# Attention probabilities normalised before the transpose, kept in fp32, and multiplied with values as the stationary operand, two heads at a time

## The reference

```python
xn = ln(x, g_norm)
q = (xn @ Wq).reshape(b, n, HEADS, DIM_HEAD).transpose(0, 2, 1, 3)
k, v = split(xn @ Wkv)                      # null key and value are put in front
sim = einsum('bhid,bjd->bhij', q, k) * SCALE + attn_bias    # bias of the null column: null_attn_bias
sim = where(causal or padding mask, neg, sim)
attn = softmax(sim, axis=-1)                # over the null column and 1024 keys
out = einsum('bhij,bjd->bhid', attn, v)
return ln(out @ Wout, g_out)                # added to x by the caller
```

## Time and profile before

| what | value |
|---|---|
| median of three runs | 1751.86 us |
| profiled execution, its own time | 1753.54 us |
| its span | 1751.1 us |
| PE busy (by modelled ends) | 1476.3 us, 84% |
| DVE busy | 1391.8 us, 79% |
| ACT busy | 1241.2 us, 71% |
| POOL busy | 752.5 us, 43% |
| mean granted TensorE clock | 0.965 of 2.4 GHz |

### The profile page before, as it was taken

The page is one execution under the profiler, slowest core; times in us unless marked ns, Lnnn a source line. Parts: engine busy times, 40 slices in busy tenths (PEclk is TensorE's granted clock), DMA queues, the critical chain, the costliest instruction groups (busy, mean ns, idle before and its releaser), DMA issues.

```text
span 1751.1 us, 46745 instructions
## 1 busy us (share of the span) xinstructions
PE 1476.3 (84%) x16377; PEld 1085.6 (62%) x16377; DVE 1391.8 (79%) x3587; ACT 1241.2 (71%) x3512; POOL 752.5 (43%) x1412
## 2 busy tenths in 40 slices
PE   2367778787889999987788888999999799999998
PEld 1255556666667777765666666777777555555555
DVE  4556677877888989977788888899999677777777
ACT  1278888888889999987888888889999533233322
POOL 5546676543433434356554332322231366522222
PEclk9668999999999999999999999999999899999999
DMA  4002111211122213111222111222223000000000
GB/s 136 14 16 62 50 61 50 79 62 52 54 74 86 86 63 109 56 38 38 72 64 74 56 67 65 73 79 86 92 98 98 2 25 19 1 1 1 13 13 25
DMA packets 50442, 96.70 MB, mean 55 GB/s; under 512 B 3332, under 2 KB 27028, under 8 KB 50212
## 3 DMA queue, kind: packets, MB, share of 16 engines
q1 hardware_dynamic: 45504, 90.27, 15.8%
q10 hardware_dynamic: 4708, 3.45, 0.7%
HBM read 91.54 MB, written 2.17 MB: 54 GB/s over the span
## 4 chain that ended last, share of the span: by engine, by line
PE 43%; DVE 19%; ACT 17%; issue 10%; POOL 2%; ACTq 0%; DVEq 0%; POOLq 0%
DVE p_lo L965 7%; PE tp L1307 7%; ACT p_hi L723 6%; DVE biased L881 4%; PE sc L1081 3%; PE sc L1082 3%; PE sc L1083 3%; ACT probs L630 3%; PE sc L1198 3%; ACT q_b L651 3%; PE sc L1199 3%; PE op L1081 2%; PE aux L1081 2%; ACT q_sq L663 2%; PE aux L1083 2%
## 5 line engine op out<-in xcount | busy, mean ns | idle before, releaser
L965 DVE TENSOR_TENSOR p_lo<-tp,p_hi 128x512 f16<-128x512 f32 (+3 forms) x768 | 416.3, 554 | 157.0 <-ACT p_hi L723 150.3
L881 DVE CUSTOM_DVE_ANT_0 biased<-sc,bias,neg_null 128x256 f32<-128x256 f32 (+7 forms) x512 | 411.0, 803 | 3.7 <-PE sc L1199 1.4
L1307 PE MATMUL tp<-ident,probs 128*128 128x128 f32 x2304 | 390.9, 279 | 26.5 <-DVE p_lo L965 23.6
L630 ACT ACTIVATE probs<-biased,neg_max 128x256 f32<-128x256 f32 (+7 forms) x512 | 397.9, 777 | 6.9 <-DVE neg_max L881 5.5
L723 ACT ACTIVATE p_hi<-tp 128x512 f16<-128x512 f32 (+3 forms) x768 | 370.2, 495 | 42.7 <-PE tp L1307 32.7
L1081 PE MATMUL op<-v_s,p_hi 128*128 128x64 f16 x2304 | 285.3, 194 | 63.3 <-DVE p_lo L965 46.2
L1307 PEld LDWEIGHTS tp<-ident,probs 128*128 128x128 f32 x2304 | 269.0, 142 | 64.0 <-issue 49.4
L1198 PE MATMUL sc<-k_a,q_a 128*128 128x512 f16 (+3 forms) x768 | 254.8, 332 | 54.0 <-DVE neg_max L881 48.0
L1083 PE MATMUL op<-v_s,p_lo 128*128 128x64 f16 x2304 | 284.3, 194 | 0.0
L1082 PE MATMUL op<-v_s,p_hi 128*128 128x64 f16 x2304 | 284.3, 194 | 0.0
L1081 PEld LDWEIGHTS op<-v_s,p_hi 128*128 128x128 f16 x2304 | 216.3, 99 | 95.2 <-DVE p_lo L965 73.7
(11 more groups left out here) (257 smaller groups left out, 3732.3 us busy)
## 6 DMA issues: line engine op xcount, KB each, us to landing
bias<-rel_table SPq DMA_DIRECT2D x4, 2048.0 KB, 8.3
bias<-in_fside_16xSxS SPq DMA_DIRECT2D x4, 2048.0 KB, 8.5
bias<-rel_table SPq DMA_DIRECT2D x4, 1792.0 KB, 8.0
bias<-in_fside_16xSxS SPq DMA_DIRECT2D x4, 1792.0 KB, 7.2
bias<-rel_table SPq DMA_DIRECT2D x4, 1536.0 KB, 7.6
bias<-in_fside_16xSxS SPq DMA_DIRECT2D x4, 1536.0 KB, 6.7
bias<-rel_table SPq DMA_DIRECT2D x4, 1280.0 KB, 5.5
bias<-in_fside_16xSxS SPq DMA_DIRECT2D x4, 1280.0 KB, 6.0
```

The lines of the kernel that those rows point to most:

```text
L630: ac.activation(probs[:, i % 2, 0:w], biased[:, i % 2, 0:w], ACT.Exp, bias=neg_max[:, u % 2, i % HU:i % HU + 1], scale=-1.0, accum_out=row ...
L881: ve.tensor_tensor_reduce(out=biased[:, i % 2, 0:w], in0=sc[i % 2][:, 0:w], in1=bias[:, g % 2, i % HU, 0:w], scale=-1.0, scalar=neg_null[: ...
L965: ve.tensor_tensor(p_lo[:, gi % 4, 0:nb * P], tp[gi % 2][:, 0:nb * P], p_hi[:, gi % 4, 0:nb * P], ALU.subtract).then_inc(s["p_lo"], 1)
L1307: last = te.transpose(tp[gi % 2][:, jj * P:(jj + 1) * P], probs[:, n % 2, (j0 + jj) * P:(j0 + jj + 1) * P], ident[:, :])
```

## The change

1. **Null column.** The null key's score is copied as one more column behind `biased` (a one-element DVE copy per step), so that the exponential and the row sum take it in. d_null, p_null, denom, o_null and o_raw are gone. The normalised null probabilities of all 16 heads are gathered in `pn`, transposed once per query tile and batch element, and multiplied with `nv_w` (null value times output weights, made once per layer) into the same accumulation as the output projection.
2. **Scaling on POOL.** DVE takes the reciprocal of each step's row sum, and POOL multiplies that step's probabilities in place before they are transposed. probs gets a third buffer.
3. **One fp32 eviction.** Each group of transposed probabilities is copied once, in fp32, into `p_t` (four buffers of a whole row), by DVE for two groups of three and by ACT for the third.
4. **Values stationary.** Values are kept in fp32. For each block and each of two heads there is one fp32 matmul with 64 columns of values as weights and the 128 transposed probabilities moving. The even head writes partitions 0 to 63 and the odd one 64 to 127, so op holds the transposed output at once, and o_n's transposes are gone. A pair of heads is multiplied in two parts, in the two slots after its second transposes.
5. **Order and buffers.** Scores run one slot further ahead, and so do bias and exponential; q's transposes move from k = 3 to k = 2. The q squares of a unit are one ACT pass and one DVE reduction. Bias is loaded two heads at a time into three buffers, and layer 1's causal select on it is done by halves.

```diff
+    def copier(self, gi):
+        return 1 if gi % 3 == 2 else 0
...
-        bias = sb("bias", [P, 2, HU, S])
+        att = sb("att", [P, 10 * S])
+        bias = att[:, 0:6 * S].rearrange("p (a h n) -> p a h n", a=3, h=2)
+        p_t = att[:, 6 * S:10 * S].rearrange("p (a n) -> p a n", a=4)
...
-        v_s = [sb(f"v_s{i}", [P, B * TILES, 2, DH], F16) for i in range(2)]
+        v_s = [sb(f"v_s{i}", [P, B * TILES, DH]) for i in range(2)]
...
     (load_bias)
-            if g >= 2:
-                eng.wait_ge(s["biased"], UNITS // HG * HU * (g - 1))
+            if q >= 3:
+                g_, p_ = divmod(q - 3, 2)
+                eng.wait_ge(s["biased"], 2 * HU * g_ + HU + 2 * p_ + 2)
...
     (gpsimd)
-                    gp.tensor_tensor(o_n[:, :, :], o_raw[:, :, :],
-                                     r_den[:, :].unsqueeze(2).to_broadcast([P, HU, DH]), ALU.mult)\
-                        .then_inc(s["o_n"], 1)
-                if k == 2 and 0 <= m + 3 < U0:
+                i = n + 1
+                if 0 <= i < N:
+                    pool.wait_ge(s["r_den"], i + 1)
...
+                    gp.tensor_tensor(pn[:, T % 2, bt, hg * HU + i % HU:hg * HU + i % HU + 1], probs[:, i % 3, w:w + 1],
+                                     r_i, ALU.mult).then_inc(s["pn"], 1)
+                    p_i = probs[:, i % 3, 0:w]
+                    gp.tensor_scalar(p_i, p_i, r_i, 1.0, ALU.mult, ALU.mult).then_inc(s["scaled"], 1)
+                if k == 3 and 0 <= m + 3 < U0:
...
     (scalar)
-                i = n + 1
+                i = n + 2
...
-                    ac.activation(probs[:, i % 2, 0:w], biased[:, i % 2, 0:w], ACT.Exp,
+                    ac.activation(probs[:, i % 3, 0:w + 1], biased[:, i % 2, 0:w + 1], ACT.Exp,
...
-                        for h in range(HU):
-                            ac.activation(q_sq[:, h, :], first[:, h * DH:(h + 1) * DH], ACT.Square,
-                                          accum_out=q_ss[:, h:h + 1]).then_inc(s["q_ss"], 1)
+                        ac.activation(q_sq[:, :, :].rearrange("p h d -> p (h d)"), first[:, 0:UW], ACT.Square)\
+                            .then_inc(s["q_sq"], 1)
...
-                        ac.activation(p_hi[:, gi % 4, 0:nb * P], tp[gi % 2][:, 0:nb * P], ACT.Copy)\
-                            .then_inc(s["p_hi"], 1)
+                        if plan.copier(gi) == 1:
+                            act.wait_ge(s["pt"], gi + 1)
+                            if n >= 4:
+                                act.wait_ge(s["pv"], n // 2 - 1)
+                            ac.activation(p_t[:, n % 4, j0 * P:(j0 + nb) * P], tp[gi % 2][:, 0:nb * P], ACT.Copy)\
+                                .then_inc(s["copy_act"], 1)
...
     (vector)
-                    ve.reciprocal(r_den[:, :], denom[:, :]).then_inc(s["r_den"], 1)
-                i = n + 2
+                i = n + 1
+                if 0 <= i < N:
+                    dve.wait_ge(s["probs"], i + 1)
+                    if i >= HU:
+                        dve.wait_ge(s["scaled"], i - HU + 1)
+                    ve.reciprocal(r_den[:, i % HU:i % HU + 1], rows[:, i % HU:i % HU + 1]).then_inc(s["r_den"], 1)
+                i = n + 3
...
+                    ve.tensor_copy(biased[:, i % 2, w:w + 1], null_i).then_inc(s["null_col"], 1)
+                if k == 2 and 0 <= m + 3 < U0:
...
+                    ve.reduce_sum(q_ss[:, :], q_sq[:, :, :], AX).then_inc(s["q_ss"], 1)
...
-                        ve.tensor_tensor(p_lo[:, gi % 4, 0:nb * P], tp[gi % 2][:, 0:nb * P],
-                                         p_hi[:, gi % 4, 0:nb * P], ALU.subtract).then_inc(s["p_lo"], 1)
+                        if plan.copier(gi) == 0:
...
+                            ve.tensor_copy(p_t[:, n % 4, j0 * P:(j0 + nb) * P], tp[gi % 2][:, 0:nb * P])\
+                                .then_inc(s["copy_dve"], 1)
...
     (tensor)
-                    last = three(o_h, p_hi[:, gi % 4, cols], p_lo[:, gi % 4, cols], v_hi, v_lo,
-                                 j == 0, j == nk - 1)
-                last.then_inc(s["pv"], 1)
+            def pv(n0, first_, last_):
+                layer, u, nk = plan.layer(n0), plan.unit(n0), plan.tile(n0) + 1
+                bt, c = u % B, n0 % HU // 2
+                if c == 0 and first_ == 0 and u >= 1:
+                    pe.wait_ge(s["ot_lo"], u)
...
+                for j in range(first_, last_):
+                    for e in range(2):
+                        if j % 4 == 0 or j == first_:
+                            copied(plan.first_group[n0 + e] + j // 4)
+                        last = te.matmul(op[e * DH:(e + 1) * DH, c * P:(c + 1) * P], v_s[layer][:, bt * TILES + j, :],
+                                         p_t[:, (n0 + e) % 4, j * P:(j + 1) * P], start=(j == 0), stop=(j == nk - 1))
...
-                i = n + 3
+                i = n + 4
...
+                        last = te.matmul(first[:, 0:D], pn_t[:, u % B, :], nv_w[:, :], start=False, stop=True)
...
+                    n0 = n // 2 * 2 - 2
+                    nk = plan.tile(n0) + 1
+                    part = (n0, 0, (nk + 1) // 2) if n % 2 == 0 else (n0, (nk + 1) // 2, nk)
...
-                        pe.wait_ge(s["probs"], n + 1)
+                        pe.wait_ge(s["scaled"], n + 1)
...
-                    if j < len(before):
-                        pv(before[j])
                     if j == 0:
                         small()
+                    if j == 0 and part and part[1] < part[2]:
+                        pv(*part)
```

325 lines of the change are left out of this document (170 added, 155 removed).

## The result

After the change the median is 1937.03 us (1935.76 to 1939.94, 4 runs) against 1752.77 (4 runs) for the kernel before: ratio 1.105, 95% interval 1.103 to 1.107, or 184 us more. The forecast was 1713 us, with a range from 1671 to 1880. The profiled execution spans 1933.2 us. In all lines PE is TensorE, PEld its weight loads, DVE VectorE, ACT ScalarE, POOL GpSimd and SPq the queue of SyncE. A window gives its length, the busy time of the five in this order, the granted clock, the DMA share and GB/s.

What follows compares the result with a forecast made beforehand. Attention, 1285 us in 512 steps, was taken as bound by each stretch's busiest engine plus waits. Busiest engine minus 11 us and waits counted at 28 made minus 39: 1714.5 profiled, 1713 median, range 1671 to 1880.

Steps and rivals of the forecast that it cites:

- Waits and DMA: Half-size bias loads cost nothing, SyncE's weight loads keep their places; a late bias load would stall POOL in layer 1.
- The array drains between widths: Rival, chance 0.08: two width changes per step on TensorE at 0.16 us each, PE +0.32, 1801 us.
- PE: the passes: TensorE's fp32 value products: two column halves side by side, 0.108 us per block against 0.088 for the fp16 ones.
- Serial passes: Rival, chance 0.28: the column halves' value passes run one after the other, 0.216 us per block, 1860 us.
- DVE: Transposed-probability copies at p_lo's price, a third of that work gone; VectorE 1.41 to 2.77 and 1.37 to 2.55 us per step.
- The one-element copy: VectorE's null-column copy, taken at 0.166 us; rival, chance 0.09: held while POOL runs, up to 0.8 us, 1876 us.
- POOL: GpSimd's scaling of probabilities: 0.205 + 0.205 us per block; other bound 0.2 + 0.4 per 256 columns.
- POOL's case as a rival: Rival, chance 0.07: POOL's queue holds layer 0, +9 us there; 1745 us, no change worth the name.
- one of my two signs of being wrong: The forecast is wrong if PE waits for POOL in layer 0.
- The output bank: At a unit's end op is held until ot_hi and ot_lo, about 0.4 us each; PE has scores and transposes in front.
- Sum: Busiest engine per stretch minus 11 us, plus 28 counted from PE's 70 us of p_lo waits: minus 39, 1713 us.
- My own test: The forecast is wrong if the stretches with 7.5 blocks grow by more than 0.2 us per step.

Runs made afterwards that it cites:

- e1: Changed kernel with SyncE's weight loads put six bias loads earlier: 1872.47 us, ratio 1.069.
- e10: e1 with each pair's value products as one full-width fp32 product per key block (values left out, output not meaningful): 1829.15 us, ratio 1.044.
- e12: e10 with three fp16 products per block of a pair in place of the fp32 product's two passes: 1805.83 us, ratio 1.032.
- e13: e12 with GpSimd scaling only four columns per head, and value products placed in one slot as in e9: 1799.50 us, ratio 1.025.
- e7: Kernel before, with SyncE's seven weight loads during attention made to wait for the step the changed kernel's loads wait for: 1804.10 us, ratio 1.029.
- e2: e1 with all of a pair's even-head value products before the odd head's, instead of alternating column halves: 1928.73 us, ratio 1.101.
- e4: e1 with GpSimd scaling only the first four probabilities of each row, the rest left unnormalised: 1856.68 us, ratio 1.059.
- e9: e1 with a pair's value products all in its first slot, but the second in layer 1's rows of 1 to 4 blocks: 1844.38 us, ratio 1.053.
- e14: e9 with VectorE's second output eviction (ot_lo) moved behind its slot's reciprocal and biased scores: 1880.86 us, ratio 1.073.
- e15: e9 with the output bank freed after one fp32 ScalarE eviction, ot_hi moved behind the exponentials and ot_lo behind the scores: 1901.61 us, ratio 1.086.
- e16: e15's eviction edit, with all of a pair's value products in its first slot in every row: 1911.52 us, ratio 1.092.
- e17: e9 with one useless 256-column fp16 product per step in rows of 1 to 3 blocks, to test the clock: 1847.00 us, ratio 1.052.
- e18: e13 with one useless 256-column fp16 product per step in rows of 1 to 4 blocks, to test the clock: 1794.86 us, ratio 1.024.

## Why the prediction was wrong

Down the chain of kernels that each take one part away:

| | median us | part |
|---|---|---|
| after | 1937.0 | |
| e1 | 1872.5 | 65 late weights |
| e10 | 1829.2 | 43 changes of width |
| e12 | 1805.8 | 23 longer passes |
| e13 | 1799.5 | 6 scaling and placing |
| before | 1752.8 | 47 left, 34 of them in short rows |

*Waits and DMA: failed.* "SP's weight loads keep their places among them" is the dearest sentence. By count of loads they do; but the bias load ahead of each (for the weights due at step 8L) now waits until 8L + 6 steps are scored, where the load in its place before waited for 8L. GpSimd asks for the first piece in slot 8L + 1, and VectorE scores the step in question in slot 8L + 2: the load is not even asked for when its user stands waiting. I followed the bias load through this (four steps, 7 us, still right: no bias load shows as a long wait) and not what stands behind it in SyncE's queue. The text even names who would stand still if something in that queue were late. Worked through, it is six stalls of about 10 us. e1 takes them out and e7 puts them into the kernel before, so this cause is shown.

*The array drains between widths: rejected, and it is what happens.* Its place, its count (two changes a step) and nearly its size were right: 0.295 us a step at TensorE, measured, for 0.32 in the sum. In rows of 8 blocks that alone is most of the 0.37 and 0.40 by which e1's steps exceed before's. What this rival had wrong is how much of it shows: e10 gives 43 us back, where it had 88 above the forecast, since a quicker TensorE waits longer for the others. The reason that I gave against it, a narrow weight load in the head with no gap ahead of it, was about the load and not about the product behind it. The Trainium skill, "TensorEngine Tiling (Array Packing)", Key Properties, has both rules. The trace agrees with the first: the halves work independently (twos 7 ns apart). It agrees with the second as far as it can tell: a change of width costs 0.145 to 0.150 us, though the records don't show that draining is what fills it.

*PE: the passes.* 0.108 a block side by side was the assumption on which most hung; it measured 0.109. Serial passes are refuted, by the starts and by e2.

*DVE: right.* The copy costs 0.688 us for four blocks, p_lo's price within a nanosecond, and VectorE's busy time came out 0.06 to 0.15 us a step under the sums. The one-element copy takes 0.138 to 0.154, though 338 of the 512 start while a scaling runs: that rival is refuted.

*POOL: mis-sized by half.* The slope is (1.122 - 0.375)/7 = 0.107 a block, not 0.205. The form was the right one, but its 0.615 for 256 columns is a mean of 16 with one of 2.593 us among them; their median is 0.482, and with 0.376, the least of the 128-column ones, that gives the measured slope. The other bound was miscounted too: 0.408 for 256 columns is 0.1 a block above 0.2, not 0.2. It hardly matters, since e4 prices all the scaling's length at 16 us or less. POOL's case as a rival did not come about either: with the weights early TensorE waits 20.7 us for the scaling in layer 0. Yet that PE waits for POOL there at all was one of my two signs of being wrong.

*The output bank: too cheap.* I set against it that TensorE has scores and transposes to put in front. But products of the next unit stand in the very slot that evicts the last one. e9 shows the bank on the path in layer 1's rows of 2 to 4 blocks, e14 in long rows, and e15 and e16 that freeing it sooner at the price of a later ot_hi loses more than it wins.

*Sum.* The 70 us of waits for p_lo did end, but others took their place: with the weights early TensorE waits 30 for the scaling, 31 for VectorE's copies and 78 for neg_max and ot_lo, where before it had 63 for neg_max and o_raw. Of the 28 that the sum took off for waits nothing shows. Summing the busiest engine of each stretch took for granted that a layout that was staged for three engines can be restaged free of charge. My own test for it failed clearly: rows of 7 and 8 blocks grew by 0.37 us a step in layer 1 (2.96 to 3.33), over the 0.2 that I had set.

**Open.** The 47 us. What is shown is where 34 of them lie (rows of 1 to 4 blocks), and that no single cause is shown: e13, with the scaling cut short and e9's placing, still has them (and still 18.5 and 32.3 us of waits for the bank), and e17 and e18 disagree on the clock. e15 and e16 show that these rows are sensitive to the order on ScalarE. Which order of the queues would win them back wasn't found. The best version with everything computed is e9, still 5% above the kernel before.
